# A linear attention's values, loaded replicated from DRAM in place of selection matmuls

## The reference

```python
def step(h, inp):
    qt, kt, vt, gt = inp
    h = h * jnp.exp(gt)[..., None] + kt[..., None] * vt[..., None, :]
    ot = jnp.einsum('bhk,bhkv->bhv', qt, h)
    return (h, ot)
```

## Time and profile before

| what | value |
|---|---|
| time, median of 3 runs | 1128.84 us |
| lowest and highest run | 1128.14 and 1132.46 us |
| profiled execution: span, first to last instruction | 1126.1 us |
| profiled execution: a time of its own | none is given beside the span |
| busy: TensorE, ScalarE, VectorE, GpSimd | 1022.0, 823.8, 644.2, 367.8 us |
| mean granted TensorE clock | 0.965 of full speed |
| DMA packets moved | 66.90 MB |

### The profile page before, as it was taken

One profiled execution on the slowest core, in us unless ns is written; L12 is line 12 of the kernel. 1 busy time (PEld: TensorE's weight loads), 2 busy tenths in 40 slices (PEclk: granted clock), 3 DMA queues, 4 the chain that ended last, 5 costly groups with the idle time before them and its releaser, 6 DMA issues.

```text
span 1126.1 us, 16648 instructions
## 1 busy us (share of the span) xinstructions
PE 1022.0 (91%) x5970; PEld 510.6 (45%) x5970; DVE 644.2 (57%) x1173; ACT 823.8 (73%) x1108; POOL 367.8 (33%) x317
## 2 busy tenths in 40 slices
PE   2799999999999999999698988898688899999998
PEld 1232333333333333333276655565255536666667
DVE  3121444526344443413464999999899999996200
ACT  2599999999999999999457767466567586555541
POOL 1000010101001010100152787798579756755100
PEclk7699999999999999999899999899799999999999
DMA  5766362635454462620101101100000222010200
GB/s 125 117 112 121 80 123 59 120 64 109 77 106 97 82 110 50 118 41 15 35 1 38 38 1 38 38 1 29 24 23 1 57 57 84 1 48 29 65 20 20
DMA packets 98780, 66.90 MB, mean 59 GB/s; under 512 B 61636, under 2 KB 84964, under 8 KB 96612
## 3 DMA queue, kind: packets, MB, share of 16 engines
q1 hardware_dynamic: 98656, 65.33, 27.9%
q10 hardware_dynamic: 24, 0.25, 0.1%
HBM read 46.41 MB, written 18.87 MB: 58 GB/s over the span
## 4 chain that ended last, share of the span: by engine, by line
PE 64%; DVE 15%; ACT 8%; POOL 5%; issue 4%; DMA 2%; SPq 2%; ACTq 0%; DVEq 0%; POOLq 0%
PE PS L1456 26%; PE PS L1441 15%; PE PS L1627 6%; DVE R L1268 6%; PE PS L1616 4%; PE PS L1490 4%; POOL R L869 3%; DVE R L1259 3%; PE PS L1385 1%; PE PS L1530 1%; DVE RB L1221 1%; PE PS L1554 1%; PE PS L1563 1%; PE PS L1371 1%; DVE R L1227 1%
## 5 line engine op out<-in xcount | busy, mean ns | idle before, releaser
L906 ACT ACTIVATE R<-PS 128x1024 f32<-128x1024 f32 x512 | 474.4, 1085 | 62.0 <-PE PS L1441 61.3
L1456 PE MATMUL PS<-R 128*32 128x512 f32 x2048 | 314.9, 610 | 1.6 <-issue 1.6
L869 POOL TENSOR_TENSOR R<-R 128x512 f32<-128x512 f32 x128 | 211.4, 1668 | 56.1 <-DVE R L1268 31.3
L1441 PE MATMUL PS<-RA 34*128 34x512 f32 x1024 | 189.8, 449 | 21.2 <-DMA RA<-QD 20.6
L1268 DVE TENSOR_TENSOR_SCAN R<-R 128x512 f32<-128x512 f32 x128 | 208.6, 1631 | 0.0
L1490 PE MATMUL PS<-RB,WR 128*128 128x512 f32 x640 | 175.3, 418 | 18.0 <-DVE R L1227 12.2
L1441 PEld LDWEIGHTS PS<-RA 34*128 34x128 f32 x1024 | 77.3, 187 | 218.6 <-issue 194.8
L1490 PEld LDWEIGHTS PS<-RB,WR 128*128 128x128 f32 x640 | 123.0, 195 | 63.3 <-DVE R L1227 14.2
L1456 PEld LDWEIGHTS PS<-R 128*32 128x32 f32 x2048 | 68.0, 108 | 105.8 <-issue 93.9
L855 POOL TENSOR_TENSOR RB<-R,RB 128x512 fp32r<-128x512 f32 x48 | 73.8, 1540 | 79.9 <-ACT RB L916 70.0
L845 POOL PARTITION_ALL_REDUCE R<-R x8 | 3.0, 374 | 290.4 <-DVE R L1108 290.4
(11 more groups left out here) (139 smaller groups left out, 1043.5 us busy)
## 6 DMA issues: line engine op xcount, KB each, us to landing
RA<-QD SPq DMA_DIRECT2D x256, 64.0 KB
QD<-RA SPq DMA_DIRECT2D x128, 64.0 KB, 2.2
RA<-QD SPq DMA_DIRECT2D x64, 128.0 KB
OD<-R SPq DMA_DIRECT2D x128, 32.0 KB, 1.9
R<-OD SPq DMA_DIRECT2D x128, 32.0 KB
VD<-RC SPq DMA_DIRECT2D x16, 256.0 KB, 2.2
RC<-VD SPq DMA_DIRECT2D x16, 256.0 KB
WP<-in_Wa SPq DMA_DIRECT2D x12, 256.0 KB, 3.2
```

The lines of the kernel that those rows point to most:

```text
L869: pool.tensor_tensor(st, st, Qc[b % 2], ALU.mult).then_inc(S["qh"], 1)
L906: act.activation(PR[u % 4], bank(2 * s, 1024), ACT.Exp, scale=SC).then_inc(S["exp"], 1)
L1441: op = pe.matmul(bank(2 * s + h), exact(KS[k][p:p + 34, gg, 128 * j:128 * j + 128]), exact(QS[k][p:p + 34, gg, :]), start=True, stop=True)
L1456: op = pe.matmul(bank(ob)[c:c + 32, :], VAF[b % 2][:, at:at + 32], PR[u % 4][:, 512 * h:512 * h + 512], start=(j == 0), stop=(j == 7), til ...
```

## The change

The values are no longer split in two parts. ScalarE copies them as they are (`v_c`, into `Vc`), SyncE writes them to DRAM in one transfer a block, and `replica` becomes a transfer that SyncE issues for each value: it reads the eight heads' rows of value v, each sixteen times, into the 128 partitions of `ST[n % 10]`, the tile in which product, scan and query then work in place. It waits for the gather that frees the tile (VectorE did before) and for product n - 5. Product n comes three steps of the stream after replica n, not one, and state, query and gather n move with it. The selection matrices, their two loads and two copies, the subtraction on VectorE, the read back of two transfers a block and PSUM banks 3 and 4 are no longer used. `ORDER` is written anew; after the last letter s both orders end in the same letters (`tdtttdtttttddtdtdtdtddtttdttttddzzzdt`, then d to the end). The lists of semaphores and of functions follow and are left out here.

```diff
 ORDER = (
...
-    "sddsstdssssdstsssssstdtttdtttttddtdtdtdtddtttdttttddzzzdtddddddddddddddddddddddd"
...
+    "sssdstsssssstdtttdtttttddtdtdtdtddtttdttttddzzzdtddddddddddddddddddddddd"
...
@@ -330,7 +330,5 @@
         for b in range(NBLK):
-            ps = self.proj(b, 2, self.count("v_r1"))
+            ps = self.proj(b, 2, self.count("v_c"))
             yield
-            self.add("v_hi", b, ps)
-            yield
-            self.add("v_r1", b)
+            self.add("v_c", b, ps)
             yield
@@ -398,3 +396,3 @@
 
-        for n in range(16 * NBLK + 6):
+        for n in range(16 * NBLK + 7):
             if n < 16 * NBLK:
@@ -402,13 +400,13 @@
                 yield
-            if 1 <= n <= 16 * NBLK:
-                self.add("product", (n - 1) // 16, (n - 1) % 16)
+            if 3 <= n < 16 * NBLK + 3:
+                self.add("product", (n - 3) // 16, (n - 3) % 16)
                 yield
-            if 2 <= n < 16 * NBLK + 2:
-                self.add("state", (n - 2) // 16, (n - 2) % 16)
+            if 4 <= n < 16 * NBLK + 4:
+                self.add("state", (n - 4) // 16, (n - 4) % 16)
                 yield
-            if 3 <= n < 16 * NBLK + 3:
-                self.add("query", (n - 3) // 16, (n - 3) % 16)
+            if 5 <= n < 16 * NBLK + 5:
+                self.add("query", (n - 5) // 16, (n - 5) % 16)
                 yield
-            if n >= 9 and n % 4 == 1:
-                m = (n - 9) // 4
+            if n >= 10 and n % 4 == 2:
+                m = (n - 10) // 4
                 self.add("gather", m // 4, m % 4)
@@ -541,12 +539,4 @@
                 pass
-        C0 = B0 - 3072
-        with nc.sbuf_tensor("below_c", [128, C0], F32):
-            with nc.sbuf_tensor("RC", [128, B0 - C0], F32R) as RC:
-                pass
-        with nc.sbuf_tensor("below_s", [128, NR - 512], F32):
-            with nc.sbuf_tensor("RS", [128, 512], F32R) as RS:
-                pass
         R = sb("R", [128, NR])
 
-        SPREAD = [WR[:, 1, 10, :].rearrange("p (v m) -> p v m", v=4), RS[:, :].rearrange("p (v m) -> p v m", v=4)]
         used, stop = [0], [NR]
@@ -611,12 +601,6 @@
         ST = [carve(512) for _ in range(NS)]
-        assert used[0] <= C0
-        used[0] = C0
-        RV = [carve(1024).rearrange("p (v t) -> p v t", v=2) for _ in range(2)]
-        Vp = carve(1024).rearrange("p (i t) -> p i t", i=2)
-
-        def partC(ap):
-            return exact(ap, (RC, C0, B0 - C0))
+        Vc = carve(512)
 
         W12 = bo4[:, 0, :]
-        VD = nc.dram_tensor("VD", [NBLK, 2, 8, 16, 512], F32).ap()
+        VD = nc.dram_tensor("VD", [NBLK, 8, 16, 512], F32).ap()
 
@@ -769,4 +753,2 @@
                 need.wait_ge("xt2", 7)
-                for i, at in enumerate((ST[6], ST[7])):
-                    sp.dma_start(at.rearrange("p (v m) -> p v m", v=4), io["spread"][:, 4 * i:4 * i + 4, :]).then_inc(S["c_in"], 16)
                 sp.dma_start(ST[8][0:16, 0:128], io["Wgk1"]).then_inc(S["c_in"], 16)
@@ -778,12 +760,14 @@
             def v_out(b):
-                need.wait_ge("v_r1", b + 1)
-                for i in range(2):
-                    sp.dma_start(VD[b, i, :, :, :].rearrange("h v t -> (h v) t"), partC(Vp[:, i, :]).bitcast(F32)).then_inc(S["v_out"], 16)
-                need.wait_ge("v_out", 32 * (b + 1))
-                if b >= 2:
-                    need.wait_ge("replica_ps", 16 * (b - 1))
-                for i in range(2):
-                    sp.dma_start(partC(RV[b % 2][64 * i:64 * i + 64, :, :]).bitcast(F32),
-                                 bass.AP(VD.tensor, VD[b, i, 0, 0, 0:1].offset,
-                                         [[512, 8], [8192, 8], [4096, 2], [1, 512]])).then_inc(S["rv_in%d" % (b % 2)], 16)
+                need.wait_ge("v_c", b + 1)
+                sp.dma_start(VD[b, :, :, :].rearrange("h v t -> (h v) t"), Vc).then_inc(S["v_out"], 16)
+
+            def replica(b, v):
+                n = 16 * b + v
+                need.wait_ge("v_out", 16 * (b + 1))
+                if n >= NS:
+                    need.wait_ge("gather_ps", (n - NS) // 4 + 1)
+                if n >= 5:
+                    need.wait_ge("kv", n - 4)
+                sp.dma_start(ST[n % NS], bass.AP(VD.tensor, VD[b, 0, v, 0:1].offset,
+                                                 [[8192, 8], [0, 16], [1, 512]])).then_inc(S["rep_in%d" % (n % 5)], 16)
 
@@ -934,12 +918,8 @@
                 need.wait_ge("xt2", 8)
-                need.wait_ge("c_in", 48)
-                for at, raw in zip(SPREAD, (ST[6], ST[7])):
-                    op = act.activation(at, raw.rearrange("p (v m) -> p v m", v=4), ACT.Copy)
-                op.then_inc(S["spread"], 1)
 
-            def v_hi(b, ps):
+            def v_c(b, ps):
                 need.wait_ge(*ps)
                 if b:
-                    need.wait_ge("v_out", 32 * b)
-                act.activation(partC(Vp[:, 0, :]), bank(6), ACT.Copy).then_inc(S["v_hi"], 1)
+                    need.wait_ge("v_out", 16 * b)
+                act.activation(Vc, bank(6), ACT.Copy).then_inc(S["v_c"], 1)
 
@@ -1243,6 +1223,2 @@
 
-            def v_r1(b):
-                need.wait_ge("v_hi", b + 1)
-                dve.tensor_tensor(partC(Vp[:, 1, :]), bank(6), partC(Vp[:, 0, :]), ALU.subtract).then_inc(S["v_r1"], 1)
-
             def decay_2(b):
@@ -1254,7 +1230,5 @@
                 n = 16 * b + v
-                need.wait_ge("replica_ps", n + 1)
+                need.wait_ge("rep_in%d" % (n % 5), 16 * (n // 5 + 1))
                 need.wait_ge("k_c", b + 1)
-                if n >= NS:
-                    need.wait_ge("gather_ps", (n - NS) // 4 + 1)
-                dve.tensor_tensor(ST[n % NS], bank(3 + v % 2), Kc[b % 2], ALU.mult).then_inc(S["kv"], 1)
+                dve.tensor_tensor(ST[n % NS], ST[n % NS], Kc[b % 2], ALU.mult).then_inc(S["kv"], 1)
 
@@ -1543,3 +1517,3 @@
                 need.wait_ge("xt2", 8)
-                need.wait_ge("c_in", 48)
+                need.wait_ge("c_in", 16)
                 room(6)
@@ -1557,11 +1531,2 @@
 
-            def replica(b, v):
-                n, bk = 16 * b + v, 3 + v % 2
-                room(bk)
-                need.wait_ge("rv_in%d" % (b % 2), 32 * (b // 2 + 1))
-                need.wait_ge("spread", 1)
-                pe.matmul(bank(bk), SPREAD[v % 8 // 4][:, v % 4, :], partC(RV[b % 2][:, v // 8, :]), start=True,
-                          stop=True).then_inc(S["replica_ps"], 1)
-                emptied[bk] = ("kv", n + 1)
-
             def gather(b, q):
@@ -1656,5 +1621,2 @@
             hot[p, j, 8 * j + p // 16] = 1.0
-    spread = np.zeros((128, 8, 128), np.float32)
-    for p in range(128):
-        spread[p, p % 64 // 8, 16 * (p % 8):16 * (p % 8) + 16] = 1.0
     bd = (head[:, None] == head[None, :]).astype(np.float32)
@@ -1672,3 +1634,3 @@
                         g["L1_attn_Wo"][perm, :]], axis=1),
-        "Wgk1": g["L1_attn_Wgk1"].T, "Wgk2": g["L1_attn_Wgk2"], "spread": spread,
+        "Wgk1": g["L1_attn_Wgk1"].T, "Wgk2": g["L1_attn_Wgk2"],
         "cC": np.stack([g["L1_attn_bgk2"], g["L1_attn_g_norm_w"][val]], axis=1), "hot": hot, "bd": bd,
```

More of the change, by code:

```diff
@@ L23 @@
 ORDER = (
[L24 to L33, removed]
-    "sddsstdssssdstsssssstdtttdtttttddtdtdtdtddtttdttttddzzzdtddddddddddddddddddddddd"
+    "abcbbccbbccbbbacccbbbbbbbbacbbbbcacbcbcccbcapcbbcpbpbcpcppbpcpbcppbpppssssssbcssbcbscssssppsbssssbbp"
+    "sssbbcsbbsbsspsccpbscsbscssspsssbpsssccsbspsssbspcpsssbpcssspcsscsccssbssssssscsscbsssbpsssspscbcspp"
+    "sssssssspcssspsbscsscpsssssbpptsssscsptsscsbbssstpspscsssststcssstcbsstsbssbsctsscppsscbbstsbsssssts"
+    "pbbscbstbbcspssssscscbspcbstssbsssscssscststsscsssstsbssssscctsssssstspscscsssbpcsbttscssctsssbtcsss"
+    "spstsptpsssstsbcsssspsptbsscppssstcstsssssstbtspcsbppsbspptsscssssssppspsbtpssstsstpctbsssscsbsptssp"
+    "sbstcscssbtcstcsbsbtsctbtsbcsstcbssssbtssscssscpcbsscssbstcsbssstspcscscpssssssbsssstcspttsssbssssss"
+    "tsbsssststsssssssscsspssttsttssbsscbtsppsctsptstbscssbsscssstststptcpcsssszsszssstzssstsdspdstssdsts"
+    "spddsssssddspstsssssssptpsdssttspdsssssssszsssspsdssppdssstttstsdtdtsssssdsssststsppsdspsssspsspssss"
+    "pdspsspsssssppsdssztspptpstdsssspstpsssdssstssssztstssdttssstddsssstssdsstdssstssstsdsssssssdstttsst"
+    "ssssddsssstsdstdtssdsssssdsdssstsssstssdstsssttsdsszttdtsssszsstsssstsssdtsddtstdssssssszssssddsstds"
+    "sssdstsssssstdtttdtttttddtdtdtdtddtttdttttddzzzdtddddddddddddddddddddddd"
 )
@@ L475 @@
 hi lo lo_pool gate_ps up_ps tanh gated gated_up hid_ps gelu down_ps x2 xt3_ps xt3 s_scaled
-c_in spread w12 proj_c_ps v_hi v_r1 v_out rv_in0 rv_in1 g_sum g_abs q_c decayed k_c replica_ps kv scanned carried
+c_in w12 proj_c_ps v_c v_out rep_in0 rep_in1 rep_in2 rep_in3 rep_in4 g_sum g_abs q_c decayed k_c kv scanned carried
 x4_in qh gather_ps heads mean_ps rms inv_rms tanh_c swish gate_o scaled_o out_c_ps x3 xt4_ps xt4 pooled route_ps route_act logits_r
@@ L806, in _ @@
```

(8 more changed lines are left out.)

## The result

The changed kernel takes 1196.89 us (median of 4 runs, 1194.95 to 1205.58) against 1128.49 before: a ratio of 1.062 with a 95% interval of 1.058 to 1.066, 68 us slower. The direction was forecast; the size, 36 us, was not, and 1196.89 lies at the very end of the range.

What follows compares the result with a forecast made beforehand. VectorE was taken to bound the scan's stretch. The terms +40 + 2.9 - 2.9 - 4.7 - 0.6 + 2 = +36.7 us, on a span of 1126.1 with the runs' median 2.7 above it, gave 1165 us, range 1124 to 1197.

Steps and rivals of the forecast that it cites:

- The product's meeting with GpSimd: In the scan's stretch: the product, now with two SBUF inputs, meets GpSimd's queries, +40 us, besides +2.9 for the product alone.
- The count of cover: For the product's meeting with GpSimd: less other VectorE work hides GpSimd's turns, 0.91 lost a value instead of 0.57, +44 us.
- the mean of the other two-input operations: Upper bound on the product's meeting: 38 two-SBUF operations average 1126 ns, 0.434 us over 692; 55.5 us for 128 products.
- The whole-instruction rule: Two-SBUF-input VectorE and SBUF-reading GpSimd instructions exclude each other throughout; the forecast found the rows agreeing in kind, not length.
- The rival built on it: Scan, query and product exclude one another for full length; stretch at least 472 us, time 1187 us; chance 0.08.
- The loads: On SyncE's queue: replica loads delayed by what stands in front, +2 us, bounds 0 and +16; the ring's wait 0.
- TensorE's relief: 128 replica matmuls removed, 71.0 us busy; only VectorE's two waits for TensorE credited, -2.9 us.
- The start: Before the first product: the value is ready sooner, but the product still needs ScalarE's copy of the keys; -0.6 us.
- The subtraction: On VectorE: one subtraction a block removed, seven of them in the scan's stretch, -4.7 us.
- The tail: After the last query: same written order and no TensorE backlog carried in, so change 0, again 94 us.
- The signs: Product mean 0.95 to 1.1 us, maximum near 1.7; stretch near 450; VectorE over 95% busy; load waits under 5 us.
- the faster rival: Meeting with GpSimd is conserved: -5.3 us, or -26 with VectorE's waits given back; middle -14, 1115 us; chance 0.11.

Runs made afterwards that it cites:

- ring15: The changed kernel with the ring of tiles at 15 in place of 10; 1189.68 us, ratio 1.055.
- before_two_sbuf: The kernel before with its product multiplying decays and keys, both in SBUF, in place of PSUM and keys; 1184.54 us, ratio 1.049.
- loads_eighth: The changed kernel with each replica's load cut to 64 of 512 columns and the product formed of decays and keys; 1188.23 us, ratio 1.053.
- the fastest kernel: The changed kernel with decays and keys in PSUM, ring at 15 and the order of steps of the kernel before; 1103.31 us, ratio 0.979.

## Why the prediction was right in kind and wrong in size

- **What bounds the kernel:** right. VectorE set the end of the scan's stretch before and after. Taking 71 us of matmuls off TensorE gave nothing; its busy time in the stretch didn't even fall (364.5 against 363.7 us, 76% where I expected 65%). The granted clock there fell from 0.96 to 0.86, and the same matmuls took longer, here those of the feed-forward from about 618 us on, before and after:

```profile
L1490 PE MATMUL PS<-RB,WR 128*128 128x512 f32 x468 | 128.8, 416 | 6.0 <-POOL RB L855 2.7 <-DVE R L1227 1.5 <-ACT RB L928 0.9
```

```profile
L1464 PE MATMUL PS<-RB,WR 128*128 128x512 f32 x464 | 142.4, 458 | 22.1 <-DVE R L1207 7.1 <-DVE RB L1201 5.3 <-ACT RB L912 5.3
```

- **Where the miss lies:** the span grew by 67.0 us, the sum had 36.7. Of the 30 us between, 12 are product and scan (55.1 against 42.9), 14 are VectorE's idle time (+13.4 against -0.9) and 4 the tail.
- **The product's meeting with GpSimd:** the mechanism was right, and this is the term that was mis-sized. I took +40 and +2.9, 42.9 in all. Product and scan together grew by 44.4 + 10.7 = 55.1 us in the changed kernel and by 62.7 in the kernel before with that one operand changed. The step that failed is "the waits that product and scan share should pack a little better". The closing run of scans in ring15 shows the opposite (VectorE, then GpSimd; start us, length, what):

```profile
1078.37 1.70 DVE L1233 TENSOR_TENSOR R<-R 128x512 f32<-128x512 f32 x1
1079.99 2.29 DVE L1242 TENSOR_TENSOR_SCAN R<-R 128x512 f32<-128x512 f32 x1
1082.19 1.69 DVE L1233 TENSOR_TENSOR R<-R 128x512 f32<-128x512 f32 x1
```

```profile
1077.27 14.49 POOL L853 TENSOR_TENSOR R<-R 128x512 f32<-128x512 f32 x8
```

  One value takes 3.82 us (1078.37 to 1082.19), where it was 2.15. The product waits 1.03 us (1.70 against 0.67) and the scan behind it 1.1 us (2.29 against 1.19) as well. GpSimd did eight queries in 14.49 us, 1.81 each, so it gets two turns in one value's 3.82 us: in this stretch, where queries had piled up, one before each of VectorE's two instructions. The closing run of before_two_sbuf has the same durations (1.70 and 2.29). A count per value as mine, with one turn of GpSimd to each, comes out too low where it has work in store; how much of the 12 us that makes over the whole stretch wasn't counted. The count of cover (+44) and the mean of the other two-input operations (+55.5), which I had kept as upper bound, were both nearer than the value I chose; the nearest row was the bound.
- **The whole-instruction rule** of the Trainium skill (SBUF — State Buffer, Who interferes with whom). The runs agree with its kind: with one operand in PSUM the product's maximum is 690 ns and the scan's 1283, with all of GpSimd's queries still there. As to its length, each wait in the closing run is 1.0 to 1.1 us, less than the query's 1.26. The rival built on it ended at 1187 us, nearer than my forecast, and its floor for the stretch, 472 us, is close to what came (478.6, in ring15 474.4, in before_two_sbuf 470.3, which lies below it). Waits of 1.0 to 1.1 us speak against the full length. How much of the stretch the shared path was taken, and so whether it or VectorE's own work is the bound there, wasn't settled.
- **The loads, +2, bounds 0 and +16:** wrong. VectorE waited 14.1 us for them and TensorE 12.5 for zone weights; ring15 gave back 7 us of the time, loads_eighth 9. I had read the lead off the order (three values, 9 us) and put the ring's wait at 0, "covered as long as GpSimd lags by less than three values". That is the step that failed here. A gather frees four tiles, and the first replica that needs one of them stands at the gather's own step (10 for value 10), so its lead is three steps only if the gather is done at once, and every delay of the gather shortens it. SyncE waited for a gather 30 times, with 32 gathers in all; only five products then had to wait for their loads:

```profile
SPq L771 <- PE PS L1538: 214.6, 30, 15.0
```

  GpSimd's lag isn't the only thing that counts: at the 8.1 us near the end the gather stood behind 7.41 us of zone matmuls on TensorE. And what waited behind the replica included zone loads, which I had only considered as obstacles in front.
- **TensorE's relief, -2.9:** not got. VectorE's idle time rose by 13.4 us, and with the loads' waits gone (ring15) it is still 28.0 us against 23.8.
- **The order of steps:** not priced at all. I took the new one as equal except for the tail. With the keys in PSUM it costs 13 us, with the decays there about 10.
- **The start, -0.6:** -1.5. **The subtraction, -4.7:** gone, as said. **The tail, 0:** +3.6, from the late zone loads.
- **The signs:** the product's mean (1016 ns) and maximum (1779) came as written. The stretch was 478.6 us and not near 450. The scan's mean rose to 1.71 us, VectorE was busy 92% and not over 95%, its waits for loads were 14.1 us and not under 5, and the query didn't grow.
- **Slips in the working:** an issue of SyncE was put at 0.4 us, though the pair of L786 in the earlier trace rows has 1.23 us for two, and a replica's load takes 0.574; the middle of the faster rival, between -5.3 and -26, is -16 and not -14. Neither changes the outcome.

In sum, by the runs: about 50 to 56 us for the operand and 7 to 9 for late loads. The order's share is 10 to 13 us in the variants where it could be measured, and open in the changed kernel itself. So these don't simply add up.

## What to carry to other kernels

When a change moves an operand of VectorE from PSUM (where matmuls leave their results) to SBUF, look whether GpSimd reads SBUF at the same time, and compare the minimum and maximum, not the median, of two-SBUF-input instructions already there: their spread shows the price. Freed PSUM banks can hold one input of a VectorE instruction; here the longest one, which was not the one that had been changed, gained most. A transfer that has to wait for a buffer holds up everything behind it in its queue, so its lead should be read from the buffer's release and not from its place in the order.

## What the runs showed of the hardware that was not expected

- A tensor_tensor_scan with its decay in PSUM ran as fast as from SBUF alone (1189 ns at least, 1191 with both in SBUF), and none of the 128 took more than 1283.
- In the closing runs of ring15 and before_two_sbuf, where queries had piled up, GpSimd's wide operations and VectorE's took turns: two queries in one product-scan pair, 3.8 us in place of 1.19 + 0.67.
- The 256 KB loads took SyncE 0.574 us each to issue, not the 0.35 to 0.46 us of the plain ones; the old reads of L786 took 0.588. The write of a block's values (256 KB now, two halves before) took 5.1 us to land at the median, up to 9.4, where a write took 2.2 before.
- The mean granted TensorE clock in the scan's stretch was 0.96 before, 0.86 after the selection matmuls were gone, and 0.94 in the fastest kernel, which lacks them too. In before_two_sbuf, which keeps them all, it was 0.93.
